# One fused eight-stage kernel on one core: inputs of the recurrence reordered on two queues, fillers on TensorE, and the order of one quantiser in chunk 2

## The reference

```
# layer 0
h   = GRU over the 32 tokens, first state cond        # r, z, n gates; W_ih, W_hh 256 x 768
x   = x + attention(h)                                # 16 heads of 128, rms norm on q and k, causal
y   = depthwise causal convolution of x, taps cond
x   = x + bit_linear(rms_norm(silu(bit_linear(y, w_gate)) * bit_linear(y, w_up)), w_down)
# layer 1
x   = x + attention(attention with scale and shift(x, cond))
y   = depthwise causal convolution of x
h   = relu(y @ quantised(w_fc).T);  x = x + (h * h) @ quantised(w_proj).T
```

```
i_r, i_z, i_n = split(x @ W_ih + b_ih);  h_r, h_z, h_n = split(h @ W_hh + b_hh)
r = sigmoid(i_r + h_r);  z = sigmoid(i_z + h_z);  n = tanh(i_n + r * h_n)
h = (1 - z) * n + z * h
```

## Time and profile before

| | us |
|---|---|
| median of three runs | 1351.13 |
| the runs | 1350.63 to 1352.35 |
| the profiled execution | 1351.93 |
| its span | 1350.1 |
| TensorE busy | 1293.5 (96%) |
| VectorE busy | 1138.8 (84%) |
| ScalarE busy | 800.3 (59%) |
| GpSimd busy | 85.0 (6%) |

### The profile page before, as it was taken

How to read it: one execution, slowest core, us unless ns; L and a number is a source line. 1 busy time by engine, 2 the same in 40 slices (tenths; PEclk the granted TensorE clock), 3 DMA queues, 4 the chain that set the end, 5 groups by cost and what they waited for, 6 DMA issues and landing times.

```text
span 1350.1 us, 25840 instructions
## 1 busy us (share of the span) xinstructions
PE 1293.5 (96%) x9838; PEld 951.0 (70%) x9838; DVE 1138.8 (84%) x2960; ACT 800.3 (59%) x1554; POOL 85.0 (6%) x88
## 2 busy tenths in 40 slices
PE   5999999999999999999999879899999999999998
PEld 2444444688778888888887656676777778787867
DVE  4799999789988989898979798578788888889885
ACT  3999999864646565656665644535454545555323
POOL 0000000101020101101011000000000000000000
PEclk9999999999999999999999999999999999999999
DMA  9433343611202020201122300000000000000000
GB/s 378 127 76 79 79 102 90 192 48 48 64 9 80 1 80 3 78 25 55 48 84 106 123 16 1 25 17 17 1 25 0 25 1 24 7 12 9 8 1 24
DMA packets 26535, 73.69 MB, mean 55 GB/s; under 512 B 3992, under 2 KB 5156, under 8 KB 25136
## 3 DMA queue, kind: packets, MB, share of 16 engines
q1 hardware_dynamic: 25840, 71.10, 16.9%
q10 hardware_dynamic: 576, 0.98, 0.2%
HBM read 49.26 MB, written 22.81 MB: 53 GB/s over the span
## 4 chain that ended last, share of the span: by engine, by line
PE 57%; DVE 30%; ACT 8%; issue 4%; DMA 1%; SPq 0%; DVEq 0%; ACTq 0%
DVE work L1874 11%; PE psum L995 8%; PE psum L964 7%; PE psum L589 6%; PE psum L753 4%; PE psum L1009 4%; PE psum L1037 3%; PE psum L636 3%; PE psum L560 2%; PE psum L569 2%; PE psum L910 2%; PE psum L976 2%; PE psum L688 1%; PE psum L989 1%; PE psum L944 1%
## 5 line engine op out<-in xcount | busy, mean ns | idle before, releaser
L636 PE MATMUL psum<-h_all,w_big 128*128 128x256 f32 x1024 | 235.2, 382 | 2.2 <-ACT work L1316 2.2
L636 PEld LDWEIGHTS psum<-h_all,w_big 128*128 128x128 f32 x1024 | 190.0, 190 | 33.3 <-issue 5.7
L1874 DVE SCALAR_TENSOR_TENSOR work<-work,taps 128x248 f32<-128x248 f32 (+30 forms) x558 | 148.7, 346 | 0.0
L589 PE MATMUL psum<-w_big,h_all 128*64 128x512 f32 x512 | 121.1, 595 | 0.0
L964 PE MATMUL psum<-work,w_big 128*128 128x256 f32 x512 | 118.0, 379 | 0.5 <-DVE gru_mem L2479 0.5
L753 PE MATMUL psum<-w_big,gru_mem 128*128 128x256 f32 x512 | 115.3, 383 | 0.5 <-ACT gru_mem L1362 0.5
L753 PEld LDWEIGHTS psum<-w_big,gru_mem 128*128 128x128 f32 x512 | 98.0, 192 | 15.4 <-ACT gru_mem L1362 0.6
L995 PE MATMUL psum<-w_big 128*128 128x256 f32 x448 | 106.5, 388 | 2.1 <-ACT w_big L1613 2.1
L964 PEld LDWEIGHTS psum<-work,w_big 128*128 128x128 f32 x512 | 96.0, 190 | 13.5 <-DVE gru_mem L2479 0.9
L995 PEld LDWEIGHTS psum<-w_big 128*128 128x128 f32 x448 | 84.3, 192 | 21.0 <-issue 5.9
L2477 DVE TENSOR_TENSOR gru_mem<-psum,trig 128x256 f32<-128x256 f32 x128 | 53.9, 421 | 40.9 <-PE psum L964 36.9
(11 more groups left out here) (348 smaller groups left out, 2564.4 us busy)
## 6 DMA issues: line engine op xcount, KB each, us to landing
value_rows<-w_emb SPq DMA_DIRECT2D x128, 128.0 KB, 2.3
work<-value_rows SPq DMA_DIRECT2D x16, 1024.0 KB, 5.9
w_big<-in_Wq SPq DMA_DIRECT2D x2, 2048.0 KB, 16.7
w_big<-in_Wo SPq DMA_DIRECT2D x2, 2048.0 KB, 21.4
...
w_big<-in_Wv SPq DMA_DIRECT2D x1, 2048.0 KB, 18.0
w_big<-in_Wk SPq DMA_DIRECT2D x1, 2048.0 KB, 23.9
```

What stands on the lines that cost most here:

```text
L589: mm = pe.matmul(bank(4 + n)[j * B:(j + 1) * B, :], h_all[:, k, :, 2 * pair + j], w_big[:, 2, k * H * HD + n * 512:k * H * HD + (n + 1) * ...
L636: mm = pe.matmul(bank(n % 2)[:, o * TA:(o + 1) * TA], w_big[:, s, k * H * HD + at:k * H * HD + at + HD], h_all[:, k, bass.ds(i * BA, BA), ...
L1874: ins = dve.scalar_tensor_tensor(dst[:, :, lag:], src[:, :, :T - lag], tap, dst[:, :, lag:], ALU.mult, ALU.add)
```

## The change

*Queues.* SP begins with `x_steps` of steps 0 to 3, one half of `W_ih` and one half of `W_hh` (384 KB each); then w5's first piece and its rest as before. Four of the small tables (`trig`, `cols`, `kmask`, `shrink_tab`) and `Wv` now come ahead of the rest of `x_steps`; `ln_row` comes behind it. ScalarE issues the biases, the other half of `W_ih`, `taps`, and the other half of `W_hh`.

*TensorE.* 24 fillers ahead of the wait for `gru_in`. In step 0 the x product starts the accumulation, and the bias product is added behind it, so the wait for the biases moves behind the x product. In steps 0 and 1 six fillers stand ahead of the turn.

*ScalarE.* `absolute(0)` moves ahead of the loop; in step 0 one `raised` stands behind the first tanh, two behind the second, and one behind the kept state.

*VectorE.* `piece_in(0)`, with its wait, moves ahead of the loop. The wait for `w5_in` moves from step 0 to step 1, the one for the five small tables and the three operations behind it to step 2. `rest_out` moves from the end of chunk 1 into chunk 2, between `hidden` of half 0 and of half 1.

```diff
--- before.py
+++ after.py
@@ -406,18 +406,17 @@
 
         @block.sync
         def _(sp):
-            for dst, src in ((bias_f, "gru_bias"), (pick_f, "bias_pick")):
-                sp.dma_start(dst, io[src]).then_inc(bias_in, 16)
-            for dst, src in ((w_ih, io["W_ih"]), (x_steps[:, :, 0:4 * B], io["x_steps"][:, :, 0:4 * B])):
-                sp.dma_start(dst, src).then_inc(gru_in, 16)
+            sp.dma_start(x_steps[:, :, 0:4 * B], io["x_steps"][:, :, 0:4 * B]).then_inc(gru_in, 16)
+            sp.dma_start(w_ih[:, 0:1, :], io["W_ih"][:, 0:1, :]).then_inc(gru_in, 16)
+            sp.dma_start(w_hh[:, 0:1, :], io["W_hh"][:, 0:1, :]).then_inc(hid_in, 16)
             sp.dma_start(w5[:, 0:PC], io["w5"][:, 0:PC]).then_inc(w5_first_in, 16)
             sp.dma_start(w5[:, PC:LAST_AT], io["w5"][:, PC:LAST_AT]).then_inc(w5_in, 16)
+            for dst, src in ((trig[:], "trig"), (cols[:, 0:12], "cols"), (kmask[:], "kmask"), (shrink_tab[:], "shrinks")):
+                sp.dma_start(dst, io[src]).then_inc(const_in, 16)
+            sp.dma_start(w_big[:, 2, :], io["Wv"]).then_inc(wv_in, 16)
             sp.dma_start(x_steps[:, :, 4 * B:], io["x_steps"][:, :, 4 * B:])\
                 .then_inc(steps_in, 16)
-            for dst, src in ((trig[:], "trig"), (cols[:, 0:12], "cols"), (ln_row, "ln_row"),
-                             (kmask[:], "kmask"), (shrink_tab[:], "shrinks")):
-                sp.dma_start(dst, io[src]).then_inc(const_in, 16)
-            sp.dma_start(w_big[:, 2, :], io["Wv"]).then_inc(wv_in, 16)
+            sp.dma_start(ln_row, io["ln_row"]).then_inc(const_in, 16)
             for j, src in enumerate(("Wq", "Wk")):
                 sp.dma_start(w_big[:, j, :], io[src]).then_inc(wqk_in, 16)
             sp.dma_start(w_big[:, 3, :], io["Wo"]).then_inc(wo_in, 16)
@@ -552,13 +551,19 @@
 
             def input_part(t):
 
-                for j in range(2):
+                for j in range(2 if t else 0):
                     pe.matmul(bank(t % 2)[of_half(j), :], bias_pick[:, j * B:(j + 1) * B], bias_rows,
                               start=True, stop=False, skip_group_check=True)
                 for k in range(KD):
                     for j in range(2):
                         pe.matmul(bank(t % 2)[of_half(j), P:4 * P], x_steps[:, k, t * B:(t + 1) * B],
-                                  w_ih[:, k, j * 3 * P:(j + 1) * 3 * P], start=False, stop=False, skip_group_check=True)
+                                  w_ih[:, k, j * 3 * P:(j + 1) * 3 * P], start=(t == 0 and k == 0), stop=False,
+                                  skip_group_check=True)
+                if t == 0:
+                    pe.wait_ge(bias_on.sem, 2)
+                    for j in range(2):
+                        pe.matmul(bank(0)[of_half(j), :], bias_pick[:, j * B:(j + 1) * B], bias_rows,
+                                  start=False, stop=False, skip_group_check=True)
 
             def hidden_part(t):
                 if t:
@@ -593,10 +598,10 @@
                     mm.then_inc(v_sum.sem, 1)
 
             pe.wait_ge(const_on.sem, 1)
-            pe.wait_ge(bias_on.sem, 2)
-            pe.wait_ge(gru_in, 16 * 2)
+            keep_clock(24)
+            pe.wait_ge(gru_in, 16 * 3)
             input_part(0)
-            pe.wait_ge(hid_in, 16 * 2)
+            pe.wait_ge(hid_in, 16 * 3)
             for t in range(T):
                 pair, half = t // 2 - 1, t % 2
                 hidden_part(t)
@@ -611,6 +616,8 @@
                 if t >= 2:
                     value_tile(pair, 2 * half)
                     value_tile(pair, 2 * half + 1, range(0, 1))
+                else:
+                    keep_clock(6)
                 turn_state(t)
                 if t >= 2:
                     value_tile(pair, 2 * half + 1, range(1, KD))
@@ -1215,8 +1222,11 @@
 
         @block.scalar
         def _(act):
-            for dst, src in ((w_hh, "W_hh"), (taps, "condT")):
-                act.dma_start(dst, io[src]).then_inc(hid_in, 16)
+            for dst, src in ((bias_f, "gru_bias"), (pick_f, "bias_pick")):
+                act.dma_start(dst, io[src]).then_inc(bias_in, 16)
+            act.dma_start(w_ih[:, 1:2, :], io["W_ih"][:, 1:2, :]).then_inc(gru_in, 16)
+            act.dma_start(taps, io["condT"]).then_inc(hid_in, 16)
+            act.dma_start(w_hh[:, 1:2, :], io["W_hh"][:, 1:2, :]).then_inc(hid_in, 16)
             for dst, src in ((h_rows[:, 0, :], "cond_rows"), (ident[:], "ident")):
                 act.dma_start(dst, io[src]).then_inc(rows_in, 16)
             act.wait_ge(const_on.sem, 7)
@@ -1262,25 +1272,21 @@
                 act.activation(lower, lower, ACT.Square)
                 act.activation(upper, upper, ACT.Square, bias=less_col[:]).then_inc(sq_on.sem, 1)
 
+            absolute(0)
             for t in range(T):
                 u = t - 1
                 act.wait_ge(hid_sum.sem, t + 1)
                 act.activation(gates, bank(t % 2)[:, RZ], ACT.Tanh, scale=0.5).then_inc(rz_on.sem, 1)
-                if t:
-                    raised(t, range(0, 1))
+                raised(t, range(0, 1))
                 act.wait_ge(cand_in.sem, 2 * t + 2)
                 act.activation(cand, cand, ACT.Tanh).then_inc(cand_on.sem, 1)
                 if u >= 2:
                     keep_values(u // 2 - 1, u % 2)
-                if t:
-                    raised(t, range(1, 2))
+                raised(t, range(1, 2) if t else range(1, 3))
                 act.wait_ge(h_turned.sem, t + 1)
                 act.activation(h_all[:, :, :, t], bank(2)[:, t % 2 * P:(t % 2 + 1) * P].rearrange("p (k b) -> p k b", k=KD),
                                ACT.Copy).then_inc(h_kept.sem, 1)
-                if t == 0:
-                    absolute(0)
-                    raised(0, range(0, 2))
-                raised(t, range(2, GROUP))
+                raised(t, range(2 if t else 3, GROUP))
                 if t >= 2:
                     squares(t - 2)
                 from_top(t)
@@ -2052,12 +2058,11 @@
                                                    ALU.mult, ALU.add)
                 ins.then_inc(rest_on.sem, 1)
 
+            dve.wait_ge(w5_first_in, 16)
+            piece_in(0)
             for t in range(T):
                 u = t % 2
                 q = t // NG
-                if t == 0:
-                    dve.wait_ge(w5_first_in, 16)
-                    piece_in(0)
                 dve.wait_ge(rz_on.sem, t + 1)
 
                 dve.scalar_tensor_tensor(cand, gates[:, 0:P], 1.0, bank(u)[:, HN], ALU.add, ALU.mult)\
@@ -2082,8 +2087,9 @@
                     errors(t - 3)
                 if t:
                     round_off(t - 1, not (t % NG == 3 and q >= 1 or t % NG == 0 and q >= 2))
-                if t == 0:
+                if t == 1:
                     dve.wait_ge(w5_in, 16)
+                if t == 2:
                     dve.wait_ge(const_in, 16 * 5)
                     gain_on.raised_by(dve.tensor_scalar(cols[:, GK0:GK0 + 1], cols[:, GK0:GK0 + 1], cols[:, GK0 + 1:GK0 + 2],
                                                         HD ** -0.5, ALU.mult, ALU.mult))
@@ -2260,7 +2266,10 @@
                         conv(c, lags, x_t, y_t, xt_on, 1, conv_on, cols[:, B0:B0 + KD])
 
                 if tail:
-                    hidden(c - 1, 0, (0, 1))
+                    hidden(c - 1, 0, (0,))
+                    if i == 2:
+                        rest_out()
+                    hidden(c - 1, 0, (1,))
                     weigh(c - 1, 0)
                     quantise_hidden(c - 1, 0, tail_link, lambda: last_errors(i - 3) if i > 2 else last_begin())
                     hidden(c - 1, 1, (0,))
@@ -2309,7 +2318,6 @@
                 if ffn and not tail:
                     ternary(0)
                     ternary(1)
-                    rest_out()
                 if tail:
                     if i - 2 < NG:
                         last_group(i - 2)
```

## The result

| | median, us | range, us | executions | profiled span, us |
|---|---|---|---|---|
| before | 1350.79 | 1350.19 to 1352.35 | 6 | 1350.1 |
| changed | 1361.11 | 1359.10 to 1362.17 | 6 | 1359.4 |

The ratio is 1.0075, 95% interval 1.0064 to 1.0085: the changed kernel is slower, by 10 us. Three of the six executions of the kernel before are those with the median 1351.13, from which the prediction started. The prediction was 1348.1, range 1345.4 to 1350.6, with a chance of 0.07 for slower. It was wrong in sign, and no rival named the cause.

The account below looks back on a forecast made before the run. TensorE was taken to set the recurrence's pace after a DMA-bound first 10 us, VectorE the chain behind chunk 2's conv. 1351.93 - 3.9 (opening) + 0.9 (chunk 2) = 1348.9, by the median 1348.1; range 1345.4 to 1350.6.

Parts of the forecast that it names:

- The idle products: Opening, TensorE: the 24 fillers cost nothing under the DMA wait; six at step 1 cost 0 to 0.7 us, 0 taken.
- First gates 13.6: Opening, step 0: first gates at 13.6 us instead of 15.56, a gain of 2.0, set by `w5`'s first piece landing.
- `W_hh` at 10.1: Opening: the half of `W_hh` on SP's queue, last of the first step's needs, lands at about 10.1 us.
- Step 0 to step 1, 3.48: Opening: gates of step 0 to hidden product of step 1 stay 3.48 us; TensorE then ends last, gain 3.65.
- The clock given back, 1.05: Opening, step 1: a TensorE wait in step 0 brings half clock, costing up to 1.3 us, 1.05 taken.
- rival 2: Opening: the clock holds because the gap is only 2 us; gain 4.95, time 1347.1 us, chance 0.25.
- The moved transfers: Opening: `Wv` lands at about 20.5 us, the rest of `x_steps` at 25, `ln_row` at 26, all in time.
- the slower rival: Step 2: VectorE's wait for small tables includes a late `ln_row`, decisive after 31.6 us; bound 1357.3 us, chance 0.07.
- Chunk 2, +0.9: Chunk 2: GpSimd delays the quantiser, TensorE waits 3.5 us, half clock follows; conv 0.9 us later, bounds 0 and 1.5.
- rivals 1 and 3: Chunk 2: 1, clock holds, 1347.2 us, chance 0.13; 3, GpSimd doesn't hold the quantiser, 1346.2 us, chance 0.07.
- three of three: TensorE: each of its three longest waits inside the kernel (3.4, 2.4, 2.4 us) was followed by half clock.
- The slower side: Whole kernel: chance 0.07 of being slower, resting on `ln_row` landing late at step 2.

Follow-up runs that it names:

- e2: The kernel before with only the 36 idle products added (24 at the start, six in each of steps 0 and 1): 1357.24 us, ratio 1.0037.
- k2: The changed kernel with `rest_out` back at the end of chunk 1 and without the 24 idle products at the start: 1350.03 us, ratio 0.9988.
- k3: k2 with VectorE's wait for `cond_rows` and `ident` moved behind `piece_in(0)`: 1347.92 us, ratio 0.9974.
- g2: The kernel before with 60 idle products added, 48 at the start and six in each of steps 0 and 1: 1356.81 us, ratio 1.0043.
- e4: The kernel before with only `rest_out` moved to its new place in chunk 2: 1354.26 us, ratio 1.0014.

## Why the prediction was wrong, step by step

- **The idle products, "24 at the start ... stand under the wait for the DMA: nothing".** This is the step that failed and turned the sign. True where it looked: they are covered in the opening (they end at 6.11, the inputs release TensorE at 6.34), and the two sixes too (0.83 each, no wait of the turn on them). Wrong 280 us later: their 72 instructions moved a border of TensorE's program to the end of a run of scores, and its piece wasn't there. That cost a stop of 3.34 and half clock behind it, 4.8 us between 264 and 366 us, and with it came the late value store (0.7). In e2 the idle products alone cost 5.9 by the medians, net of 2.2 of gain, so about 8; in its profiled execution it is about 6 (span 1353.9 for 1350.1). The kernel before's page has a line for the queue of instructions, and the prediction read nothing from it.
- **First gates 13.6: measured 17.19.** The bytes ahead of `w5`'s piece were counted, and it landed even earlier (9.2 for 11.1). What was left out is the wait ahead of `piece_in(0)`: VectorE waits there for `cond_rows` and `ident`, and `ident` landed at 14.7 instead of 8.65. The rule for moved transfers, to look at every waiter of each, was applied to `ln_row` and not to these. Worth 1.7 (k2 against k3).
- **`W_hh` at 10.1: measured 12.5.** The prediction took the half on SP's queue as the last; that one was there at 7.4, and the one on ScalarE's, issued at 2.67, took 9.8 us for 384 KB. The prediction had weighed the Trainium skill, page "DMA: Bandwidth & Descriptors", section "Issuing engines are not separate DMA queues" (transfers of all issuing engines interleave on the same 16 DMA engines), with no row to judge it. This trace agrees in so far as the second queue brought nothing sooner: its half landed 9.8 us after issue, its equal on the first queue 5.2, though fewer bytes stood ahead of it on its own queue (478 KB against 640).
- **Step 0 to step 1, 3.48, and the gates of step 1 right behind the product:** right in form. 17.19 to 20.57 is 3.38, and the gates came at 22.20, with the product done at 22.15 (before, they had waited 1.74 for ScalarE).
- **The clock given back, 1.05:** didn't happen. The hidden products of steps 1 and 2 took 1.58 each, as in rival 2. The fall came one step earlier, behind the 4.32 us wait for `W_hh` (the product took 2.77). The opening gave 28.61 - 27.13 = 1.5 instead of 3.9.
- **The moved transfers:** right. `Wv` landed at 19.6 (predicted 20.5), the rest of `x_steps` at 24.0 (25, issued at 6.5) and `ln_row` at 25.3 (26, issued at 7.1); no engine waited for them, and the slower rival didn't occur. In g2, where the kernel before's order stands, VectorE's wait for the small tables reached 7.3 us and step 2's gates came at 28.88, with nothing left of the opening's gain.
- **Chunk 2, +0.9:** the mechanism was right in each link, and in the changed kernel and e4 rivals 1 and 3 did not occur. The size was off: 3.0 (e4), 2.3 between 366 and 393 us in the changed kernel. `head_rms` took 6.41, not 5.43, so L2228 came at 382.07 (predicted 381.25 to 381.8). TensorE waited 4.30 and not 3.5, L753 started at 385.91, 0.8 behind before's 385.12 where I had it 0.4 ahead, and took 9.08, not 8.76. So TensorE was 0.8 + 2.0 = 2.8 late, not 1.3, and by 399 us VectorE was 2.8 late as well, not 0.9. The prediction's "three of three" for the fall of the clock behind a long wait of TensorE isn't a rule: in k2 and k3 the clock held behind the same 2.44 us.
- **The slower side** was held at 0.07, for a transfer that turned out harmless. An edit that only adds instructions had no rival of its own.
